# First attention of a two-layer decoder: key sums in 32-column groups, output products at a head's end

## What is computed

```python
qkv = jnp.einsum('bsh,hf->bsf', x, w_qkv)
scores = jnp.einsum('bhqd,bhkd->bhqk', q, k) / jnp.sqrt(jnp.float32(D_HEAD))
probs = jax.nn.softmax(scores, axis=-1)
values = jnp.einsum('bhqk,bhkd->bhkd', probs, v)
out = jnp.einsum('bsf,fh->bsh', values, w_o)
...
x = _layernorm(x + _L0_attn_ref(x, L0_attn_w_qkv, L0_attn_w_o), axis=-1)
```

## Time and profile before

| what | before |
|---|---|
| median of 3 runs | 846.15 us (845.87 to 847.85) |
| the profiled execution | 848.14 us |
| its span | 846.3 us |
| PE busy in the span | 782.1 us (92%) |
| DVE, ACT, POOL busy | 538.5, 359.8, 373.7 us |
| PE's granted clock, mean | 0.969 of full |
| the first attention, scores of head 0 to last output product | 17.3 to about 241.3 us |

### The profile page before, as it was taken

One profiled execution on the slowest core, in us unless ns is written; L12 is line 12 of the kernel. 1 busy time (PEld: TensorE's weight loads), 2 busy tenths in 40 slices (PEclk: granted clock), 3 DMA queues, 4 the chain that ended last, 5 costly groups with the idle time before them and its releaser, 6 DMA issues. The chain is left out here.

```text
span 846.3 us, 12715 instructions
## 1 busy us (share of the span) xinstructions
PE 782.1 (92%) x4092; PEld 599.9 (71%) x4092; DVE 538.5 (64%) x1049; ACT 359.8 (43%) x843; POOL 373.7 (44%) x339
## 2 busy tenths in 40 slices
PE   7899999999969889999999997988887896999997
PEld 5788888888844457888888885754445343788886
DVE  4666666677678964333333357799984698864535
ACT  3555555555541062232323234368884001543422
POOL 2221212123118924656565643799972885521100
PEclk9999999999989979999999999999999897999999
DMA  9210101010201014433333340000000012000001
GB/s 317 65 51 25 50 25 50 25 50 27 68 13 43 20 58 112 131 112 107 112 107 116 90 121 10 1 2 1 2 2 1 25 50 69 0 16 17 1 1 50
DMA packets 27054, 45.24 MB, mean 53 GB/s; under 512 B 3424, under 2 KB 16608, under 8 KB 26752
## 3 DMA queue, kind: packets, MB, share of 16 engines
q1 hardware_dynamic: 27008, 44.65, 17.7%
HBM read 43.45 MB, written 1.18 MB: 53 GB/s over the span
## 5 line engine op out<-in xcount | busy, mean ns | idle before, releaser
L1479 PE MATMUL bank<-xTh,ringh 128*128 128x512 f32 x420 | 169.5, 403 | 0.6 <-DVE xTl L1150 0.6
L1480 PE MATMUL bank<-xTl,ringh 128*128 128x512 f32 x420 | 166.2, 396 | 0.0
L1481 PE MATMUL bank<-xTh,ringl 128*128 128x512 f32 x420 | 166.0, 395 | 0.0
L1219 DVE TENSOR_TENSOR arena<-bank,arena 128x512 f32<-128x512 f32 x48 | 33.2, 691 | 114.9 <-ACT arena L881 105.7
L1481 PEld LDWEIGHTS bank<-xTh,ringl 128*128 128x128 f32 x420 | 79.3, 189 | 18.9
L1479 PEld LDWEIGHTS bank<-xTh,ringh 128*128 128x128 f32 x420 | 79.6, 190 | 16.7 <-issue 1.6
L1480 PEld LDWEIGHTS bank<-xTl,ringh 128*128 128x128 f32 x420 | 79.5, 189 | 15.1
L632 POOL TENSOR_TENSOR arena<-arena 128x512 f32<-128x512 f32 x48 | 62.6, 1303 | 51.6 <-DVE HTl L1223 49.5
L881 ACT ACTIVATE arena<-bank 128x512 f32<-128x512 f32 x48 | 28.7, 598 | 126.1 <-PE bank L1481 126.0
L555 POOL CAST ringh<-ring 128x768 fp32r<-128x768 f32 x15 | 12.7, 846 | 152.4 <-DMA ring<-w_attn 149.4
L1517 PE MATMUL bank<-outh,HTh 128*128 128x256 f32 x192 | 54.9, 286 | 3.1 <-DVE outl L1064 1.2
(11 more groups left out here) (269 smaller groups left out, 1971.7 us busy)
## 6 DMA issues: line engine op xcount, KB each, us to landing
ring<-w_moe SPq DMA_DIRECT2D x24, 256.0 KB, 2.9
arena<-route SPq DMA_DIRECT2D x16, 384.0 KB, 4.1
ring<-w_attn SPq DMA_DIRECT2D x15, 384.0 KB, 3.2
toep<-toep SPq DMA_DIRECT2D x32, 128.0 KB, 2.1
arena<-route SPq DMA_DIRECT2D x16, 256.0 KB, 4.1
outring<-w_down SPq DMA_DIRECT2D x24, 128.0 KB, 2.1
outring<-wo_attn SPq DMA_DIRECT2D x16, 128.0 KB, 2.0
arena<-route SPq DMA_DIRECT2D x16, 128.0 KB, 4.0
```

The lines of the kernel that those rows point to most:

```text
L1219: dve.tensor_tensor(H1[:, i % LAG, :], bank[:, 1 + i % 2, :], SG[:, i % 2, :], ALU.mult).then_inc(gu_done, 1)
L1479: pe.matmul(o, ringh[:, slot, wc], xTh[:, k, halves[j]], start=(k == 0), stop=False)
L1480: pe.matmul(o, ringh[:, slot, wc], xTl[:, k, halves[j]], start=False, stop=False)
L1481: ins = pe.matmul(o, ringl[:, slot, wc], xTh[:, k, halves[j]], start=False, stop=(k == DK - 1))
```

## The change

The key sums are formed from the unscaled exponentials. The reciprocals of the row sums, repeated 32 times along the free axis (`inverse`, from `invert` on DVE), become the stationary operand, and the exponentials in plain fp32 the moving one: `sum_keys` issues eight products of 128x128 onto 32 columns, one a sequence, into the four 32-partition groups of bank 2. ACT copies them out (`evac_key_sums`), SP sends one partition of each group to DRAM, waits until that has landed, and spreads the 1024 sums over all partitions with a second transfer (`spread_key_sums`). DVE scales the values of head h - 1 in head h, behind both row maxima. On PE the output products go to the end of a head, and the key sums stand once between projection groups 4 and 5. The rescaling of the probabilities, Eh, El and the matrix of ones remain for the last head alone.

```diff
@@ -451,10 +457,26 @@
...
+            def spread_key_sums(h, slot):
+                sp.wait_ge(ks_evac, h + 1)
+                settle(sp, sp_settled)
+                if not isinstance(h, int) or h >= 2:
+                    sp.wait_ge(sums_moved[slot], 16 * (h - slot))
+                    settle(sp, sp_settled)
+                    sp.wait_ge(vc_done, 2 * (h - 1))
+                    settle(sp, sp_settled)
+                sp.dma_start(sums_out[slot, :].rearrange("(j g s) -> g j s", j=2, g=4),
+                             key_sums[::32, slot, :].rearrange("g (j s) -> g j s", j=2)).then_inc(sums_moved[slot], 16)
+                sp.wait_ge(sums_moved[slot], 16 * (h - slot) + 16)
+                settle(sp, sp_settled)
+                sp.dma_start(spread_sums[:, slot, :], sums_out[slot, :].partition_broadcast(P)).then_inc(sums_moved[slot], 16)
...
             def load_attn0(h, slot):
...
+                if not isinstance(h, int) or h >= 2:
+                    spread_key_sums(h - 2, slot)
@@ -472,7 +494,9 @@
...
-            with sp.Fori(1, NH // 2) as i:
+            load_attn0(2, 0)
+            load_attn0(3, 1)
+            with sp.Fori(2, NH // 2) as i:
@@ -506,6 +530,7 @@
...
+            spread_key_sums(NH - 2, 0)
@@ -785,15 +810,14 @@
...
             def exps(h, j):
...
-                act.wait_ge(el_done, count(2 * (h - 1) + j + 1))
+                act.wait_ge(ks_done, count(h))
...
             def high_e(h, j):
-                act.wait_ge(en_done, 2 * h + j + 1)
-                act.wait_ge(csum_done, count(2 * (h - 1) + j + 1))
+                act.wait_ge(en_done, j + 1)
@@ -809,25 +833,33 @@
...
+            def evac_key_sums(h, slot):
+                act.wait_ge(ks_done, h + 1)
+                if not isinstance(h, int) or h >= 2:
+                    act.wait_ge(sums_moved[slot], 16 * (h - slot))
+                act.activation(key_sums[:, slot, :], bank[:, 2, 0:2 * S], ACT.Copy).then_inc(ks_evac, 1)
...
             def head(h, slot):
...
+                exps(h, 0)
...
-                else:
-                    high_out(h, slot, out0_done, count(h - 1))
-                exps(h, 0)
-                if not last:
...
-                high_e(h, 0)
-                high_e(h, 1)
-                if not last:
+                if not isinstance(h, int) or h > 0:
+                    high_v(h - 1, 0)
+                    high_v(h - 1, 1)
+                if last:
...
-                high_v(h, 0)
-                high_v(h, 1)
-                if not last:
-                    evac_v(h + 1, 1 - slot, 0)
-                    evac_v(h + 1, 1 - slot, 1)
+                    high_e(h, 0)
+                    high_e(h, 1)
+                    high_v(h, 0)
+                    high_v(h, 1)
+                    return
+                evac_key_sums(h, slot)
+                evac_v(h + 1, 1 - slot, 0)
+                evac_v(h + 1, 1 - slot, 1)
+                high_out(h, slot, out0_done, count(h - 1))
@@ -1039,6 +1071,11 @@
...
+            def invert(h, j):
+                dve.wait_ge(exp_done, 2 * h + j + 1)
+                dve.reciprocal(inverse[:, 4 * j:4 * j + 4, :], rowsum[:, 4 * j:4 * j + 4].unsqueeze(2).broadcast_to([P, 4, 32]))\
+                    .then_inc(rinv_done, 1)
...
             def recip(h, j):
@@ -1065,32 +1102,46 @@
...
             def scale_v(h, slot, j):
-                dve.wait_ge(csum_done, 2 * h + j + 1)
+                half = slice(j * HALF, (j + 1) * HALF)
+                if isinstance(h, int) and h == NH - 1:
+                    dve.wait_ge(csum_done, j + 1)
+                    sums = bank[:, 2 + j, :]
+                else:
+                    dve.wait_ge(sums_moved[slot], 16 * (h - slot) + 32)
+                    sums = spread_sums[:, slot, half]
...
-                dve.tensor_tensor(VTc[:, j * HALF:(j + 1) * HALF], bank[:, 2 + j, :],
-                                  VT[:, slot, j * HALF:(j + 1) * HALF], ALU.mult).then_inc(vc_done, 1)
+                dve.tensor_tensor(VTc[:, half], sums, VT[:, slot, half], ALU.mult).then_inc(vc_done, 1)
...
             def head(h, slot):
...
+                first = isinstance(h, int) and h == 0
...
+                if not first:
+                    scale_v(h - 1, 1 - slot, 0)
+                    scale_v(h - 1, 1 - slot, 1)
...
+                    low_v(h - 1, 0)
+                    low_v(h - 1, 1)
...
-                recip(h, 0)
-                recip(h, 1)
-                low_e(h, 0)
-                if not last:
-                    evac_k(h + 1, 1 - slot, 0)
-                low_e(h, 1)
-                if not last:
-                    low_out(h, slot)
-                scale_v(h, slot, 0)
-                if not last:
-                    evac_k(h + 1, 1 - slot, 1)
-                low_v(h, 0)
-                scale_v(h, slot, 1)
-                low_v(h, 1)
+                    recip(h, 0)
+                    recip(h, 1)
+                    low_e(h, 0)
+                    low_e(h, 1)
+                    scale_v(h, slot, 0)
+                    low_v(h, 0)
+                    scale_v(h, slot, 1)
+                    low_v(h, 1)
+                    return
+                evac_k(h + 1, 1 - slot, 0)
+                invert(h, 0)
+                invert(h, 1)
+                evac_k(h + 1, 1 - slot, 1)
+                if not first:
+                    low_v(h - 1, 0)
+                    low_v(h - 1, 1)
+                low_out(h, slot)
@@ -1498,7 +1549,10 @@
             def scores(h, slot, j):
...
-                pe.wait_ge(vc_done, count(2 * h - 1 + j))
+                if j == 0:
+                    pe.wait_ge(ks_evac, count(h))
+                else:
+                    pe.wait_ge(exp_done, count(2 * h))
@@ -1507,10 +1561,20 @@
...
             def key_weights(h, j):
...
-                pe.wait_ge(el_done, 2 * h + j + 1)
+                pe.wait_ge(el_done, j + 1)
...
+            def sum_keys(h):
...
+                pe.wait_ge(rinv_done, 2 * h + 2)
+                for j in range(2):
+                    for g in range(4):
+                        b = 4 * j + g
+                        ins = pe.matmul(bank[32 * g:32 * (g + 1), 2, j * S:(j + 1) * S], inverse[:, b, :],
+                                        E[:, b * S:(b + 1) * S], start=True, stop=True)
+                ins.then_inc(ks_done, 1)
...
             def out_products(o, xh, xl, wh, wl, first, final):
@@ -1557,18 +1621,19 @@
                 scores(h, slot, 0)
                 ahead(0)
                 scores(h, slot, 1)
-                ahead(1)
+                if isinstance(h, int) and h == NH - 1:
+                    attn_out(h - 1, 1 - slot)
+                    pe.wait_ge(act_evac, 4 * NH)
+                    conv(0, 0, 0)
+                    key_weights(h, 0)
+                    key_weights(h, 1)
+                    return
+                for c in range(1, 5):
+                    ahead(c)
+                sum_keys(h)
+                ahead(5)
                 if not isinstance(h, int) or h > 0:
                     attn_out(h - 1, 1 - slot)
-                ahead(2)
-                if isinstance(h, int) and h == NH - 1:
-                    pe.wait_ge(act_evac, 4 * NH)
-                    conv(0, 0, 0)
-                key_weights(h, 0)
-                ahead(3)
-                key_weights(h, 1)
-                ahead(4)
-                ahead(5)
 
             def project_first(c):
                 part, j = c // 2, c % 2
```

More of the change, by code:

```diff
@@ L240, in decoder_layers @@
         E = take(TOK)
+        key_sums = take(2 * 2 * S).rearrange("p (s n) -> p s n", s=2)
+        spread_sums = take(2 * TOK).rearrange("p (s t) -> p s t", s=2)
+        inverse = take(B * 32).rearrange("p (b c) -> p b c", b=B)
+        sums_out = nc.dram_tensor("sums_out", (2, TOK), F32, kind="Internal").ap()
         outh = sb("outh", [P, 2, D], F32R)
@@ L312, in decoder_layers @@
         en_done = sem("en_done")
+        ks_done = sem("ks_done")
+        ks_evac = sem("ks_evac")
+        sums_moved = [sem("sums_moved0"), sem("sums_moved1")]
         eh_done = sem("eh_done")
@@ L356, in decoder_layers @@
         u_done = sem("u_done")
-        r_done = sem("r_done")
         silu_done = sem("silu_done")
@@ L1050, in low_e @@
             def low_e(h, j):
-                dve.wait_ge(eh_done, 2 * h + j + 1)
+                dve.wait_ge(eh_done, j + 1)
                 half = slice(j * HALF, (j + 1) * HALF)
```

## The result

The prediction was wrong. It said 844.7 us and a range up to 851.5; the kernel became slower. Medians and intervals here and in the experiments leave out single executions that were far slower than the rest of the same kernel.

What follows compares the result with a forecast made beforehand. PE's issue was taken to bound the middle heads. Middle heads -4.2, head 0 -3.45 and last head +6.15 sum to -1.5 us; against the 846.15 median this gives 844.7 us, range 840.5 to 851.5.

Steps and rivals of the forecast that it cites:

- who could come late: Middle heads: with output products moved, DVE and ACT evacuations still fit between PE's groups; no wait, 0.14 us to spare.
- Transfers: Key sums to DRAM and back, hidden by 2.3 us; next projection weights some microseconds later, against PE's lead of about nine.
- small waits: Middle heads before: average 13.96 us against 13.92 in the head read, waits mostly for El, gone after the change.
- (c): Middle heads: reciprocals outlast 1.02 us, PE waits before each last projection group; 6.3 us worse, 851.0 us; chance 0.15.
- (d): Middle heads: transfers of the sums land later than a head allows; 850 to 858 us; chance 0.08.
- (e): Key-sum group on PE: column groups not side by side, 1.61 us instead of 0.58; 860 us; chance 0.05.
- Head 0: First head: no stop for El, 10.79 us, then 0.82 waiting for POOL's weights; gain 3.45 us.
- A middle head on PE: Key pairs out (0.94 us), 32-column group in (0.67): head 13.65 us instead of 13.92; 14 heads gain 4.2 us.
- R: Time of one widened reciprocal on DVE: 0.88 us, no wait up to 1.02.
- Transfers hidden: Middle heads: the key sums' spread lands 2.3 us before the scaling's latest start.
- The last head: Head 15: 4.6 us stop before head 14's output products, then half clock; 19.7 us against 13.54, a loss of 6.15.

Runs made afterwards that it cites:

- all three edits: Changed kernel with POOL's split behind the scalings, one reciprocal ahead of DVE's first key copy, and the last head rearranged; 844.02 us, 0.9962 of before.
- the first experiment: Changed kernel with POOL's weight split held back until DVE has scaled the values of the head before; 849.53 us, 1.0027 of before.

## Why the prediction was wrong

**The step that failed** is "who could come late". It gives the two scalings no time of their own, but its latest start for them, 5.1 us, comes out only with 0.68 each, which is DVE's row at 112.53. That row reads one source from PSUM and one from SBUF; in the change both lie in SBUF, and the scalings took up to 2.33 and, in head 6, 3.40 together. And the sentence on SP's queue under "Transfers" found that the next weights come some microseconds later, but held this only against the nine microseconds of lead of PE. It never asked where in DVE's list POOL's split would then fall. These two half-seen things meet: in head 6, split at 4.2 into the head, scaling at 4.4. The nine lengthened heads cost 133.45 - 9 x 13.81 = 9.2 us. The other three executions, 859.56 to 861.70, have no trace. In that of the kernel with the convolution first, whose middle heads are the same, head 5 is lengthened as well. If heads 2, 5 and 13 all were, by the mean of 1.02, the profiled execution would take 859.3, near the median of 859.91; that this is the difference is argued and not shown.

The trace of the kernel before held the same meeting, and the prediction passed it by. It explained the 13.96 against 13.92 by "small waits", mostly for El. Thirteen of the 14 heads take 13.91 to 13.94; the whole excess is head 13, with 14.46. There POOL was already at work for the convolution, one rescaling with both sources in SBUF took 1.29 instead of 0.69, ended 0.55 behind POOL's instruction, and PE waited for El. DVE, then POOL:

```profile
206.68 1.29 DVE L1047 TENSOR_TENSOR arena<-arena,rinv 128x512 f32<-128x512 f32 x1
```

```profile
204.94 2.48 POOL L590 TENSOR_TENSOR lowraw<-cT 128x512 f32<-128x512 f32 x2
```

The Trainium skill states the rule, page "SBUF — State Buffer", section "Who interferes with whom": a DVE instruction with two SBUF inputs contends with a GpSimd instruction that reads SBUF, and the ports that they share are an exclusive lock. The runs agree: 0.68 for the scaling with one source in PSUM beside POOL's cast, 2.34 us for the longest with both in SBUF, 0.69 again once POOL waits.

Put into the sum, the rows of the change give 1.6 us more on DVE where one scaling meets the subtraction (2.34 against 0.69) and 2.1 where both meet POOL (3.40 against 1.29). With the reserve of 0.9 that the prediction left DVE (4.2 to 5.1), PE bears 0.7 to 1.2 of it; 1.02 was measured. This belonged among the rivals, and none of the five was it. The "slower" ones there all fell: (c) by reciprocals of 913 ns, (d) by scalings that wait for no DMA, (e) by a group of 0.57 us. That (e) named 860 us, the time that came out, is a coincidence.

**Head 0:** right. It lasts 10.96 against 10.79, there is no fall of the clock, and head 1 waits for POOL 1.01 us (0.82 predicted).

**A middle head on PE:** 13.81 against 13.65, and the size was off by 0.16. The group of key sums takes 0.57 (134.53 to 135.10 in the rows above), as in the earlier trace rows. But the last product ahead of it starts at 134.20 and needs 0.23, so PE begins the group 0.10 late, and the projection group behind it lasts 1.50 (135.10 to 136.60) instead of 1.39. The sum had 0.09 for the two changes of tile shape together; they cost 0.21. Another 0.04 lies in the four projection groups ahead. So 14 heads gain 14 x (13.956 - 13.81) = 2.0 us, not 4.2.

**R:** right. 913 ns against 0.88 predicted, below the limit of 1.02. The slope of the rows for 4, 8 and 16 results held up to 128; eight passes a result didn't show.

**Transfers hidden:** right from head 2 on, by 1.9 us in the one head read, where 2.3 was worked out. For head 1 the margin is not safe, as the trace of all three edits shows.

**The last head:** right up to the second wait, and then one term was missing. From the head's start to the output products of head 15, 247.51 - 231.28 = 16.23 against 237.90 - 227.79 = 10.11, a loss of 6.12 where 6.15 was predicted, with a stop of 4.36 and the clock at half:

```profile
237.59 0.36 PE L1581 MATMUL bank<-outh,VTch 128*128 128x256 f32 x1 [4.36 <-DVE VTcl L1096]
...
247.51 0.36 PE L1581 MATMUL bank<-outh,VTch 128*128 128x256 f32 x1 [1.80 <-DVE VTcl L1096]
```

```profile
239.00:240.00 1.00, 1.00 (x7) 0.50 0.38 130
240.00:241.00 1.00, 1.00 (x7) 0.50 0.00 1
```

But after the 1.80 us stop, the same as before, the clock fell a second time, and the output products took 252.09 - 247.51 = 4.58 instead of 3.43: 1.15 us more. What lies behind the stage gives more than that back, 2.6 us: before, the clock stood at half from about 247.4 to 257.6, around the layer norm; in the matching stretch, 10.8 us later, it is at half only from about 262 to 265.6.

**The sum with what was measured:** -4.1 for head 0, -2.0 for the price of 14 heads, +1.3 for head 1 and +9.2 for the collisions, +7.3 for the last head, -2.6 behind it, -0.8 at the start: 8.3, and the spans differ by 8.2. Without the collisions the change would still not have paid: the first experiment, 849.5, is slower than before by 0.27%, because the last head takes back what head 0 and the shorter heads give. Both faults can be mended; the kernel with all three edits is then 0.4% faster than before (0.9948 to 0.9976).

## What to carry to other kernels

When an operand moves from PSUM to SBUF, read anew what the instruction shares with other engines: the row of its old form doesn't price the new one. When a change delays one item of a queue, follow that item to the engine that consumes it, and lay its new place against everything that runs at that time, not only against its deadline. A small wait, put where the two would meet, gave back 10 us, more than any term of the estimate. And read the odd head of the trace before, not only a typical one: the same meeting stood there already.

## What was not expected of the hardware

A blocked DVE instruction ends about 0.55 us after POOL's instruction ends (0.54 to 0.56 for all thirteen lengthened scalings of the change's trace, and for the rescaling of head 13 before), little less than its whole 0.69. The other side pays too: POOL's subtraction takes 2.17 to 2.27 us beside a scaling, and 1.81 to 1.85 otherwise. One small instruction with a single SBUF source is held up as well: in head 13 before, the short instruction behind a row maximum (TENSOR_SCALAR, 128x4) took 1.81 us instead of 0.17 beside POOL's subtraction. The reciprocals of the change, also with one SBUF source, were not: 0.89 to 0.94 beside it.

PE's clock doesn't follow the length of the stop alone. After a stop of 1.80 us it stayed up before; after 1.80 it fell in the change, and after 1.79 in the kernel with the convolution first. The two kernels with the last head rearranged have nearly the same stops, 0.81, 0.75 and 1.47 in one and 0.51, 0.87 and 1.47 in the other; the profiled execution of the first keeps full clock there, that of the second falls at about 236.6, inside the last stop. The mean clock from 222 to 270 us, over which the stage ends, is 0.89 before and in the change, 0.86 in the first experiment and 0.93 in the rearranged last head.

A fall more or less in this stretch cost 1.15 us in one place of the change, and the shorter ones behind the stage gave most of 2.6 us back; a single execution says little about it. What decides a fall was not settled.
